# Attention in a macaron block: single score banks and maxima over pairs of banks

## The chip, the core and the metric

The kernel runs on one core of a Trainium2 chip. The metric is the device time of one execution in microseconds. The core has TensorE (matmul and transpose, into PSUM), VectorE, ScalarE, GpSimd and SyncE, which issues the DMAs. PSUM has eight banks; one bank holds 512 float32 columns on each of 128 partitions. PE in the profile is TensorE's matmul, PEld its weight load, DVE VectorE, ACT ScalarE, POOL GpSimd, SP SyncE.

## The reference

The input x is 4 x 2048 x 256. The block computes, in float32,

```
x = x + 0.5 * ffn(layernorm(x))      # gate/up/down with blockwise FP4 quantisation, 256 -> 704 -> 256
x = x + attention(layernorm(x))      # 16 heads of 16 columns, softmax over 2048 keys, w_out
x = x + 0.5 * ffn(layernorm(x))
```

The attention is `softmax(q k^T / 4) v` for each of 4 x 16 = 64 (batch, head) pairs, called heads below, followed by the output projection.

## The kernel before, in words

The phases run one after another: weights, norm, feed-forward, norm, projection, attention (`attend_phase`, L746), output projection, norm, feed-forward. The change lies in the attention phase alone.

Queries and keys are split into three bfloat16 parts each, stacked to 96 rows, so that one bfloat16 matmul of 96 rows gives the score nearly in float32. Three more rows of Q hold minus the maximum of each query (in three bfloat16 parts), against rows of ones in K. So each block of scores is computed twice. First, for the maxima (`unit`, L984): queries on the partitions and keys on the columns, VectorE takes the maximum of each row (L933). A head has 16 x 2048 such rows in 64 units of 128 queries x 512 keys. Later, for the softmax: keys on the partitions and queries on the columns, 99 rows deep, so that the maximum is already subtracted (L1032); ScalarE takes the exponential (L920) into `probs`, and TensorE multiplies by V (`values`, L1002), which also sums the denominators with a column of ones. Each group of scores or maxima is four matmuls with 32 columns of weights each, side by side in the array, that write 32 partitions each of one bank.

A head g goes in 16 rounds kt (128 keys each). A round on TensorE's queue follows `ORDER` (L762): four groups of scores of head g (False, c) and four maxima units of head g+1 (True, c), from round 12 on of head g+2; then the values of the round before. The maxima run LEAD = 16 units ahead. After round 13 (`NEG_AT`) `turn_neg` (L997) transposes minus the maxima of head g+1, VectorE copies them (L946), and SyncE moves them with three DMAs into the rows of Q (L841). VectorE reduces the 16 x 4 partial maxima to minus the maximum at round 11 (L939), GpSimd splits it. In every eighth head, at round 6, VectorE also inverts denominators (L142). When the values of head g-1 are complete, in round 0 of head g, ScalarE copies them from PSUM to `OT` (L912).

PSUM: `ps_s` is four banks, used as two halves of 1024 columns. A half's exponential waits until both its groups are written, and the groups of the next round wait for the exponential of the half that they overwrite. `ps_o` is one bank for the values. `ps_b` is a ring of three single banks (`RING`); each fill takes the next bank, and `take` (L977) lets TensorE wait until the fill three before has been read. The transpose is a fill of this ring too. All orders are written out by hand; each engine has one queue in program order, and semaphores count groups (`scored`), exponentials (`exped`), fills (`bank_full`, `bank_free`) and rounds of values (`pv_done`).

Of the kernel before, what the change touches and what calls it, by code (L numbers as in the profile page):

```python
# [22 lines left out]
ALU = mybir.AluOpType  # L23
ACT = mybir.ActivationFunctionType
# [5 lines left out]
P = 128  # L30
# [715 lines left out]
def attend_phase(nc, m):  # L746
    NH = B * H
    SLOTS = 3
    UNITS = 64
    LEAD = 16  # L750
    HALF = S // 2

    STRIP = 32


    RING = 3
    FILLS = UNITS + 1
    MAX_AT = 11
    NEG_AT = 13
    INVERT_AT = 6  # L760

    ORDER = ((True, 0), (False, 0), (True, 1), (False, 1), (False, 2), (True, 2), (False, 3), (True, 3))  # L762
    with ExitStack() as ctx:
        def sb(name, shape, dt=F32):
            return ctx.enter_context(nc.sbuf_tensor(name, shape, dt))
# [12 lines left out]
        neg_padded = sb("neg_parts", [P, P], BF16)  # L778
        neg_parts = neg_padded[:, 0:3 * KT].rearrange("p (a t) -> p a t", t=KT)
        neg_T = sb("neg_T", [3 * KT, P], BF16)  # L780
        ps_s = ctx.enter_context(nc.psum_tensor("ps_s", [P, 2, HALF], F32))
        ps_o = ctx.enter_context(nc.psum_tensor("ps_o", [P, 512], F32))
        ps_b = ctx.enter_context(nc.psum_tensor("ps_b", [P, RING, 512], F32))

        qk_loaded = [m.qk_loaded0] + [sem(f"qk_loaded{s}") for s in range(1, SLOTS)]
        v_ready, ones_set = sem("v_ready"), sem("ones_set")
# [20 lines left out]
        def fills_to_neg(n):  # L807

            if isinstance(n, int) and n == 0:
                return 1  # L810

            fills = (n - 1) * FILLS + FILLS_AHEAD + 4 * (NEG_AT + 1) + 1
            if isinstance(n, int) and n == NH - 1:
                fills += UNITS - LEAD - 4 * (NEG_AT + 1)
            return fills

        class Ring:
# [13 lines left out]
        def known(g, at_least):  # L831

            return not isinstance(g, int) or g >= at_least

        with nc.Block() as block:
            @block.sync
            def _(sp):
                def neg_rows(n, s):
                    sp.wait_ge(bank_free, fills_to_neg(n))
                    for k in range(3):  # L840
                        sp.dma_start(Q[s][PAIRS + k:PAIRS + k + 1, :].rearrange("o (t q) -> o t q", q=P),  # L841
                                     neg_T[k * KT:(k + 1) * KT, :]).then_inc(neg_loaded, 16)

                def body(g, s):
                    if not isinstance(g, int) or g + 2 < NH:
                        if known(g, 1):
                            sp.wait_ge(scored, g * 2 * KT)
                            load_head(sp, m, Q[(s + 2) % SLOTS], K[(s + 2) % SLOTS], g + 2, qk_loaded[(s + 2) % SLOTS])
                    if known(g, 1):
                        sp.wait_ge(o_kept, g)  # L850
                        store_head(sp, m, g - 1)
                    if known(g, 1) and g % GROUP == 0:
                        spread_denominators(sp, m, g // GROUP - 1)
                    if not isinstance(g, int) or g + 1 < NH:
                        neg_rows(g + 1, (s + 1) % SLOTS)

                for n in range(1, SLOTS):
                    load_head(sp, m, Q[n], K[n], n, qk_loaded[n])
                neg_rows(0, 0)
                heads(sp, body, lambda: None)  # L860
# [45 lines left out]
            @block.scalar  # L906
            def _(act):
                def keep_o(g):
                    act.wait_ge(pv_done, g * KT)
                    if known(g, 2):  # L910
                        act.wait_ge(m.out_moved, (g - 1) * OUT_MOVES * 16)
                    nc.scalar.copy(m.OT[:], ps_o[:]).then_inc(o_kept, 1)  # L912

                def body(g, s):
                    for kt in range(KT):
                        for half in range(2):
                            act.wait_ge(scored, g * 2 * KT + 2 * kt + half + 1)
                            if known(g, 1) or kt >= 2:
                                act.wait_ge(pv_done, g * KT + kt - 1)
                            nc.scalar.activation(probs[:, (2 * kt + half) % 4, :], ps_s[:, half, :], ACT.Exp,  # L920
                                                 scale=float(DH) ** -0.5).then_inc(exped, 1)
                        if kt == 0 and known(g, 1):
                            keep_o(g)

                heads(act, body, lambda: keep_o(NH))

            @block.vector
            def _(dve):
                def unit(ring, s, k):

                    n, bank = ring.next()
                    dve.wait_ge(bank_full, n + 1)
                    nc.vector.tensor_reduce(mx[:, s, k // 4, bass.ds(k % 4, 1)], ps_b[:, bank, :], AX.X, ALU.max).then_inc(bank_free, 1)  # L933

                def minus_max(ring, n, s):

# [4 lines left out]
                def keep_neg(ring, n):  # L941
                    at, bank = ring.next()
                    dve.wait_ge(bank_full, at + 1)
                    if known(n, 1):
                        dve.wait_ge(neg_loaded, n * 16 * NEG_LOADS)
                    nc.vector.tensor_copy(neg_T[:], ps_b[0:3 * KT, bank].bitcast(BF16)[:, 0:P]).then_inc(bank_free, 1)  # L946

                nc.vector.memset(zeros[:], 0.0).then_inc(ones_set, 1)
                nc.vector.memset(neg_padded[:], 0.0).then_inc(ones_set, 1)
# [6 lines left out]
                def body(g, s):  # L956
                    ring = ring_of(g)
                    more, more2 = (not isinstance(g, int) or g + d < NH for d in (1, 2))
                    for kt in range(KT):
                        for j in range(4):  # L960
                            k = LEAD + 4 * kt + j
                            if k < UNITS and more:
                                unit(ring, (s + 1) % SLOTS, k)
                            if k >= UNITS and more2:
                                unit(ring, (s + 2) % SLOTS, k - UNITS)
                        if kt == INVERT_AT and known(g, 1) and g % GROUP == 0:
                            invert_denominators(nc, dve, m, g // GROUP - 1)
                        if kt == MAX_AT and more:
                            minus_max(ring, g + 1, (s + 1) % SLOTS)
                        if kt == NEG_AT and more:  # L970
                            keep_neg(ring, g + 1)
# [4 lines left out]
            def _(pe):  # L976
# [7 lines left out]
                def unit(ring, n, s, k):  # L984

                    if k == 0:
                        if not known(n, SLOTS):
                            pe.wait_ge(rows_set, n + 1)
                        pe.wait_ge(qk_loaded[s], 16 * LOADS * (n // SLOTS + 1) if isinstance(n, int) else (n - s) * (16 * LOADS // SLOTS) + 16 * LOADS)
                    qt, kb = k // 4, k % 4  # L990
                    bank = take(ring)
                    for j in range(0, P, STRIP):
                        last = nc.tensor.matmul(ps_b[j:j + STRIP, bank, :], Q[s][0:PAIRS, qt * P + j:qt * P + j + STRIP],  # L993
                                                K[s][0:PAIRS, kb * 512:(kb + 1) * 512], start=True, stop=True)
                    last.then_inc(bank_full, 1)

                def turn_neg(ring, n):  # L997
                    pe.wait_ge(neg_step, (n + 1) * NEG_STEPS)
                    bank = take(ring)
                    nc.tensor.transpose(ps_b[:, bank].bitcast(BF16)[:, 0:P], neg_padded[:], m.ident_bf[:]).then_inc(bank_full, 1)  # L1000

                def values(g, s, kt):  # L1002

                    pe.wait_ge(exped, g * 2 * KT + 2 * kt + 2)
                    if kt == 0:
                        pe.wait_ge(v_ready, g + 1)
                        if known(g, 1):
# [7 lines left out]
                def body(g, s):  # L1015
# [3 lines left out]
                    for kt in range(KT):  # L1019
                        for maxima, c in ORDER:  # L1020
                            if maxima:
                                k = LEAD + 4 * kt + c
                                if k < UNITS and more:
                                    unit(ring, g + 1, (s + 1) % SLOTS, k)
                                if k >= UNITS and more2:
                                    unit(ring, g + 2, (s + 2) % SLOTS, k - UNITS)
                                continue
                            half = c // 2
                            if c % 2 == 0 and (known(g, 1) or kt >= 1):
                                pe.wait_ge(exped, g * 2 * KT + 2 * kt + half - 1)  # L1030
                            for j in range(0, P, STRIP):
                                last = nc.tensor.matmul(ps_s[j:j + STRIP, half, (c % 2) * 512:(c % 2 + 1) * 512],  # L1032
                                                        K[s][:, kt * P + j:kt * P + j + STRIP],
                                                        Q[s][:, c * 512:(c + 1) * 512], start=True, stop=True)
                            if c % 2:
                                last.then_inc(scored, 1)
                        if kt > 0:
                            values(g, s, kt - 1)
                        elif known(g, 1):
# [133 lines left out]
```

## Time and profile before

| | us |
|---|---|
| median of 3 runs | 4177.33 |
| lowest, highest | 4172.32, 4178.78 |
| the profiled execution, its own time | 4175.14 |
| its span, first to last instruction | 4173.4 |

| engine | busy us | share of the span |
|---|---|---|
| TensorE matmul (PE) | 4028.9 | 97% |
| TensorE weight load (PEld) | 2136.3 | 51% |
| VectorE (DVE) | 3715.4 | 89% |
| ScalarE (ACT) | 2449.2 | 59% |
| GpSimd (POOL) | 1105.3 | 26% |

The attention phase lies between about 860 and 3552 us. Busy time is the union of the records on an engine; consecutive instructions of one engine can overlap, so a mean duration times a count can exceed the busy time. The ends of matmuls are modelled, their starts are not. "idle before" is the time in which an engine had no record before the row, and the arrow names what released it.

### The profile page before, as it was taken

To read this page: it belongs to the slowest core of one execution; us is meant where nothing else is said; L and a number is where in the kernel's file an instruction comes from. 1 tells how busy PE (TensorE), PEld (TensorE's weight loads), DVE (VectorE), ACT (ScalarE), POOL (GpSimd) and SP (SyncE) were. 2 spreads that over 40 slices of the span, in tenths; PEclk is the share of its full clock that TensorE was granted. 3 is DMA by queue.
4 is the path that set the end of the run, shared out by engine and by line. 5 is a ranking of instruction groups with operands and counts; after the bars stand their busy time and mean duration, and the time that the engine had idled before them with its cause. 6 is when DMAs were issued, how large, how long until landed. Compare 5 with 4: busy or idle time off the path is not lost. (4 is left out here: it accounts for less than half of the span.)

```text
span 4173.4 us, 109253 instructions
## 1 busy us (share of the span) xinstructions
PE 4028.9 (97%) x46386; PEld 2136.3 (51%) x46386; DVE 3715.4 (89%) x6349; ACT 2449.2 (59%) x2764; POOL 1105.3 (26%) x1158
## 2 busy tenths in 40 slices
PE   3999999979999999999999999999999999799999
PEld 2777765534444444444444444444444443677776
DVE  7999982679999999999999999999999996699998
ACT  1222225447777777777777777777777778122222
POOL 3888862310000000000000000000000000288886
PEclk7999999989999999999999999999999999999999
DMA  3000003310010001001001101001000100100000
GB/s 133 1 1 1 1 1 111 124 41 20 29 31 29 20 29 31 29 20 40 20 29 31 29 20 40 20 29 32 28 22 27 33 26 9 34 11 21 16 16 21
DMA packets 67121, 125.52 MB, mean 30 GB/s; under 512 B 17104, under 2 KB 46160, under 8 KB 64848
## 3 DMA queue, kind: packets, MB, share of 16 engines
q1 hardware_dynamic: 66640, 118.61, 9.5%
q8 instruction: 363, 5.95, 0.6%
q14 instruction: 118, 0.97, 0.1%
HBM read 72.55 MB, written 36.31 MB: 26 GB/s over the span
## 5 line engine op out<-in xcount | busy, mean ns | idle before, releaser
L933 DVE TENSOR_REDUCE mx<-ps_b 128x1 f32<-128x512 f32 x4032 | 2500.5, 682 | 127.0 <-PE ps_b L993 15.4
L920 ACT ACTIVATE probs<-ps_s 128x1024 f32<-128x1024 f32 x2048 | 1983.9, 1021 | 688.0 <-PE ps_s L1032 687.9
L993 PE MATMUL ps_b<-w_ffn 96*32 96x512 bf16 x10752 | 1070.2, 382 | 14.0 <-DMA w_ffn<-qk_parts_dram 12.1
L1010 PE MATMUL ps_o<-probs,w_qkvT 128*32 128x512 f32 x8192 | 1064.4, 592 | 0.6 <-ACT probs L920 0.6
L1032 PE MATMUL ps_s<-w_ffn 99*32 99x512 bf16 x10752 | 942.5, 379 | 0.6 <-ACT probs L920 0.6
L542 PE MATMUL ps_gu_f<-w_ffn,zT_f 128*128 128x352 f32 x2048 | 636.2, 464 | 10.4 <-DVE h_f L447 9.5
L993 PE MATMUL ps_b<-K,Q 96*32 96x512 bf16 x5376 | 533.3, 380 | 0.2
L993 PEld LDWEIGHTS ps_b<-w_ffn 96*32 96x32 bf16 x10752 | 302.4, 96 | 428.1 <-issue 201.4
L1032 PEld LDWEIGHTS ps_s<-w_ffn 99*32 99x32 bf16 x10752 | 304.6, 97 | 412.9 <-issue 198.7
L1032 PE MATMUL ps_s<-Q,K 99*32 99x512 bf16 x5632 | 493.5, 381 | 1.7 <-ACT probs L920 1.7
L877 POOL TENSOR_TENSOR neg_parts<-neg_max,zeros 128x16 bf16<-128x16 f32 x64 | 14.1, 221 | 1815.8 <-issue 1718.2
L542 PEld LDWEIGHTS ps_gu_f<-w_ffn,zT_f 128*128 128x128 f32 x2048 | 383.6, 192 | 205.8 <-ACT zT_f L399 12.0
L1010 PEld LDWEIGHTS ps_o<-probs,w_qkvT 128*32 128x32 f32 x8192 | 261.1, 111 | 201.1 <-ACT probs L920 1.6
L552 PE MATMUL ps_dn_f<-w_ffn,hT_f 128*128 128x256 f32 x1536 | 353.0, 379 | 5.3 <-ACT hT_f L404 5.3
L552 PEld LDWEIGHTS ps_dn_f<-w_ffn,hT_f 128*128 128x128 f32 x1536 | 291.4, 190 | 65.6 <-ACT hT_f L404 6.8
L1032 PEld LDWEIGHTS ps_s<-Q,K 99*32 99x32 bf16 x5632 | 159.6, 98 | 224.1 <-issue 102.9
L399 ACT COPY zT_f<-ps_T_f 128x256 f32<-128x256 f32 x128 | 47.6, 372 | 367.7 <-PE ps_T_f L534 346.5
L993 PEld LDWEIGHTS ps_b<-K,Q 96*32 96x32 bf16 x5376 | 151.3, 96 | 204.0 <-issue 93.7
L408 ACT ACTIVATE z_f<-x_res,shift,rstd 128x256 f32<-128x256 f32 x128 | 76.7, 601 | 246.9 <-POOL z_scaled_f L490 242.0
L504 POOL TENSOR_TENSOR h_rounded_f<-h_scaled_f,h_rounder_f 128x704 f32<-128x704 f32 x128 | 215.5, 1684 | 21.9 <-DVE h_scaled_f L481 21.9
L865 POOL COPY w_qkvT<-v_then_heads 128x256 f32<-128x256 f32 x64 | 25.4, 397 | 717.3 <-PE ps_o L1010 717.3
L464 DVE TENSOR_TENSOR h_scaled_f<-h_f,h_inv_f 128x704 f32<-128x704 f32 x128 | 199.7, 1560 | 4.4
(117 smaller groups left out, 3085.4 us busy)
## 6 DMA issues: line engine op xcount, KB each, us to landing
qk_parts_dram<-qk_parts SPq DMA_DIRECT2D x96, 256.0 KB, 2.8
w_ffn<-qk_parts_dram SPq DMA_DIRECT2D x84, 192.0 KB
w_ffn<-qk_parts_dram SPq DMA_DIRECT2D x84, 128.0 KB
x_res<-in_L_attn_x SPq DMA_DIRECT2D x4, 2048.0 KB, 20.2
factor<-denom_dram SPq DMA_DIRECT2D x64, 128.0 KB, 5.1
out<-x_res SPq DMA_DIRECT2D x16, 512.0 KB, 2.7
v_then_heads<-OT SPq DMA_DIRECT2D x224, 32.0 KB
w_ffn<-qk_parts_dram SPq DMA_DIRECT2D x84, 64.0 KB
```

Source lines behind the costliest of these rows:

```text
L399: nc.scalar.copy(zT[:, 1 - q, :], ps_zT).then_inc(zT_kept, 1)
L408: nc.scalar.activation(z[:, q, :], m.x[:, i + 4, :], ACT.Identity, bias=m.shift[:, bass.ds(i + 4, 1)], scale=m.rstd[:, bass.ds(i + 4, 1)]) ...
L464: nc.vector.tensor_tensor(blocks_of(hs[:, q, :]), blocks_of(h[:]), spread(hinv[:], I), ALU.mult).then_inc(h_step, 1)
L504: nc.gpsimd.tensor_tensor(hr[:], hs[:, q, :], hM[:, q, :], ALU.subtract).then_inc(hr_ready, 1)
L542: last = nc.tensor.matmul(ps_gu[:, c, 0:HW], zT[:, q, k * P:(k + 1) * P], m.w_guT[:, k, c * HW:(c + 1) * HW], start=(k == 0), stop=(k == K ...
L552: last = nc.tensor.matmul(ps_dn[:, 1 - q, 0:D], hT[:, 1 - q, c * P:(c + 1) * P], m.w_dnT[:, c, :], start=(c == 0), stop=(c == FC - 1))
L865: nc.gpsimd.tensor_copy(V[s][:, :, 0:DH], m.va.rearrange("p (g k d) -> p g k d", k=KT, d=DH)[:, n]).then_inc(v_ready, 1)
L920: nc.scalar.activation(probs[:, (2 * kt + half) % 4, :], ps_s[:, half, :], ACT.Exp, scale=float(DH) ** -0.5).then_inc(exped, 1)
L933: nc.vector.tensor_reduce(mx[:, s, k // 4, bass.ds(k % 4, 1)], ps_b[:, bank, :], AX.X, ALU.max).then_inc(bank_free, 1)
L993: last = nc.tensor.matmul(ps_b[j:j + STRIP, bank, :], Q[s][0:PAIRS, qt * P + j:qt * P + j + STRIP], K[s][0:PAIRS, kb * 512:(kb + 1) * 512] ...
L1010: last = nc.tensor.matmul(ps_o[32 * c:32 * c + 32, :], V[s][:, kt, :], probs[:, (2 * kt + c // 2) % 4, (c % 2) * 512:(c % 2 + 1) * 512], s ...
L1032: last = nc.tensor.matmul(ps_s[j:j + STRIP, half, (c % 2) * 512:(c % 2 + 1) * 512], K[s][:, kt * P + j:kt * P + j + STRIP], Q[s][:, c * 51 ...
```

## The change

`ps_s` becomes three single banks, used in turn by the groups of scores (group number modulo 3). Each group is signalled by itself, and ScalarE takes one exponential of 512 columns a group. The ring for the maxima becomes two pairs of banks. A unit fills both banks of a pair with 128 queries x 1024 keys, by eight matmuls, and one VectorE reduce takes the two maxima of a pair. There are 32 units a head and two a round; LEAD is 8. The order of a round becomes two groups of scores, a unit, a group of scores, a unit, a group of scores, the values. The transpose takes a pair of banks of the ring and writes the first. The order of work on VectorE, GpSimd and SyncE stays, with its counts adapted.

```diff
-    UNITS = 64
-    LEAD = 16
+    UNITS = 32
+    LEAD = 8
+    S_BANKS = 3
-    RING = 3
+    RING = 2
-    ORDER = ((True, 0), (False, 0), (True, 1), (False, 1), (False, 2), (True, 2), (False, 3), (True, 3))
+    ORDER = ((False, 0), (False, 1), (True, 0), (False, 2), (True, 1), (False, 3))
-        ps_s = ctx.enter_context(nc.psum_tensor("ps_s", [P, 2, HALF], F32))
+        ps_s = ctx.enter_context(nc.psum_tensor("ps_s", [P, S_BANKS, 512], F32))
-        ps_b = ctx.enter_context(nc.psum_tensor("ps_b", [P, RING, 512], F32))
+        ps_b = ctx.enter_context(nc.psum_tensor("ps_b", [P, RING, 2, 512], F32))
...
@@ ScalarE
-                        for half in range(2):
-                            act.wait_ge(scored, g * 2 * KT + 2 * kt + half + 1)
+                        for c in range(4):
+                            at = g * 4 * KT + 4 * kt + c
+                            act.wait_ge(scored, at + 1)
                             if known(g, 1) or kt >= 2:
                                 act.wait_ge(pv_done, g * KT + kt - 1)
-                            nc.scalar.activation(probs[:, (2 * kt + half) % 4, :], ps_s[:, half, :], ACT.Exp,
-                                                 scale=float(DH) ** -0.5).then_inc(exped, 1)
+                            nc.scalar.activation(probs[:, (2 * kt + c // 2) % 4, (c % 2) * 512:(c % 2 + 1) * 512],
+                                                 ps_s[:, at % S_BANKS, :], ACT.Exp, scale=float(DH) ** -0.5).then_inc(exped, 1)
@@ VectorE, unit
-                    nc.vector.tensor_reduce(mx[:, s, k // 4, bass.ds(k % 4, 1)], ps_b[:, bank, :], AX.X, ALU.max).then_inc(bank_free, 1)
+                    nc.vector.tensor_reduce(mx[:, s, k // 2, 2 * (k % 2):2 * (k % 2) + 2], ps_b[:, bank], AX.X, ALU.max).then_inc(bank_free, 1)
@@ TensorE, unit
-                    for j in range(0, P, STRIP):
-                        last = nc.tensor.matmul(ps_b[j:j + STRIP, bank, :], Q[s][0:PAIRS, qt * P + j:qt * P + j + STRIP],
-                                                K[s][0:PAIRS, kb * 512:(kb + 1) * 512], start=True, stop=True)
+                    for half in range(2):
+                        kb = 2 * (k % 2) + half
+                        for j in range(0, P, STRIP):
+                            last = nc.tensor.matmul(ps_b[j:j + STRIP, bank, half, :], Q[s][0:PAIRS, qt * P + j:qt * P + j + STRIP],
+                                                    K[s][0:PAIRS, kb * 512:(kb + 1) * 512], start=True, stop=True)
                     last.then_inc(bank_full, 1)
@@ TensorE, values
-                    pe.wait_ge(exped, g * 2 * KT + 2 * kt + 2)
+                    pe.wait_ge(exped, g * 4 * KT + 4 * kt + 4)
@@ TensorE, a round's scores
-                            half = c // 2
-                            if c % 2 == 0 and (known(g, 1) or kt >= 1):
-                                pe.wait_ge(exped, g * 2 * KT + 2 * kt + half - 1)
+                            at = g * 4 * KT + 4 * kt + c
+                            if at >= S_BANKS:
+                                pe.wait_ge(exped, at - S_BANKS + 1)
                             for j in range(0, P, STRIP):
-                                last = nc.tensor.matmul(ps_s[j:j + STRIP, half, (c % 2) * 512:(c % 2 + 1) * 512],
+                                last = nc.tensor.matmul(ps_s[j:j + STRIP, at % S_BANKS, :],
                                                         K[s][:, kt * P + j:kt * P + j + STRIP],
                                                         Q[s][:, c * 512:(c + 1) * 512], start=True, stop=True)
-                            if c % 2:
-                                last.then_inc(scored, 1)
+                            last.then_inc(scored, 1)
```

## Rows read from the trace of the kernel before

**Rows 1.** Stretches: us, busy of PE, PEld, DVE, ACT, POOL, then clock, DMA.
```profile
2500.00:3500.00 1000.00, 999.78 (x15264) 440.83 (x15260) 955.46 (x1576) 749.50 (x787) 45.01 (x131) 1.00 0.10 27
```

**Rows 2.** Waits of weight loads, 920 to 3500: us in total, times, longest.
```profile
PEld ps_b L993 <- DVE mx L933: 8.4, 21, 0.6
```

**Rows 3.** Order of time, TensorE, one round: start, us, engine, line, operation, count.
```profile
2047.28 0.39 PE L993 MATMUL ps_b<-w_ffn 96*32 96x512 bf16 x4
...
2049.02 1.03 PE L1010 MATMUL ps_o<-probs,w_qkvT 128*32 128x512 f32 x8
2049.88 0.39 PE L993 MATMUL ps_b<-w_ffn 96*32 96x512 bf16 x4
```

**Rows 4.** Order of time around the transpose of a head.
```profile
2043.53 1.04 PE L1010 MATMUL ps_o<-probs,w_qkvT 128*32 128x512 f32 x8
...
2044.66 0.40 PE L993 MATMUL ps_b<-w_ffn 96*32 96x512 bf16 x4
2044.77 0.22 DVE L946 COPY neg_T<-ps_b 48x128 bf16<-48x128 bf16 x1
...
2045.12 15.50 DVE L933 TENSOR_REDUCE mx<-ps_b 128x1 f32<-128x512 f32 x24
```

**Rows 5.** Order of time: two copies of OT, a head apart, and the values before one.
```profile
2051.62 1.03 PE L1010 MATMUL ps_o<-probs,w_qkvT 128*32 128x512 f32 x8
...
2052.80 0.59 ACT L912 COPY OT<-ps_o 128x512 f32<-128x512 f32 x1
...
2094.74 0.59 ACT L912 COPY OT<-ps_o 128x512 f32<-128x512 f32 x1
```

**Rows 6.** Order of time in the last head, which has no maxima beside it.
```profile
3519.94 0.59 ACT L912 COPY OT<-ps_o 128x512 f32<-128x512 f32 x1
3520.41 3.81 ACT L920 ACTIVATE probs<-ps_s 128x1024 f32<-128x1024 f32 x4
...
3524.40 3.77 ACT L920 ACTIVATE probs<-ps_s 128x1024 f32<-128x1024 f32 x4 [0.18 <-PE ps_s L1032]
...
3525.47 0.21 PEld L1032 LDWEIGHTS ps_s<-Q,K 99*32 99x32 bf16 x8 [0.64 <-ACT probs L920]
```

**Rows 7.** The page's groups of instructions: busy, mean ns, idle before.
```profile
L933 DVE TENSOR_REDUCE mx<-ps_b 128x1 f32<-128x512 f32 x4032 | 2500.5, 682 | 127.0 <-PE ps_b L993 15.4
L920 ACT ACTIVATE probs<-ps_s 128x1024 f32<-128x1024 f32 x2048 | 1983.9, 1021 | 688.0 <-PE ps_s L1032 687.9
```

**Rows 8.** One line of the projection phase: ns min/median/max.
```profile
L704 DVE TENSOR_REDUCE stats<-ps_yT x32: 1223/1224/1226, 733.6 to 830.5; 128x1024 f32 x32
```

**Rows 9.** Order of time: the maximum over a head's parts.
```profile
2039.55 0.22 DVE L939 TENSOR_REDUCE neg_max<-mx 128x16 f32<-128x64 f32 x1
```

**Rows 10.** Order of time around a reciprocal of the denominators.
```profile
1228.11 0.94 DVE L142 RECIPROCAL denom<-denom 128x128 f32<-128x128 f32 x1
...
1228.97 6.10 DVE L933 TENSOR_REDUCE mx<-ps_b 128x1 f32<-128x512 f32 x10
...
1229.18 0.40 PE L1032 MATMUL ps_s<-w_ffn 99*32 99x512 bf16 x4
1229.65 0.10 PEld L993 LDWEIGHTS ps_b<-K,Q 96*32 96x32 bf16 x4 [0.57 <-DVE mx L933]
```

**Rows 11.** Order of time: the units ahead of the first head.
```profile
861.50 9.66 DVE L933 TENSOR_REDUCE mx<-ps_b 128x1 f32<-128x512 f32 x16 [12.51 <-PE ps_b L993]
...
871.61 0.62 PE L993 MATMUL ps_b<-w_ffn 96*32 96x512 bf16 x4 [1.58 <-DMA Q<-neg_T]
```

**Rows 12.** Order of time around the last transpose and the next head's first load.
```profile
3513.50 1.05 PE L1032 MATMUL ps_s<-w_ffn 99*32 99x512 bf16 x16
...
3513.85 1.80 SPq L841 DMA_DIRECT2D Q<-neg_T  x3
...
3514.38 1.03 PE L1010 MATMUL ps_o<-probs,w_qkvT 128*32 128x512 f32 x8
...
3517.14 0.13 PEld L1032 LDWEIGHTS ps_s<-Q,K 99*32 99x32 bf16 x4 [0.41 <-DMA Q<-neg_T]
```

More of the change, by code:

```diff
@@ L810, in fills_to_neg @@
                 return 1
-            fills = (n - 1) * FILLS + FILLS_AHEAD + 4 * (NEG_AT + 1) + 1
+            fills = (n - 1) * FILLS + FILLS_AHEAD + 2 * (NEG_AT + 1) + 1
             if isinstance(n, int) and n == NH - 1:
-                fills += UNITS - LEAD - 4 * (NEG_AT + 1)
+                fills += UNITS - LEAD - 2 * (NEG_AT + 1)
             return fills
@@ L846, in body @@
                         if known(g, 1):
-                            sp.wait_ge(scored, g * 2 * KT)
+                            sp.wait_ge(scored, g * 4 * KT)
                             load_head(sp, m, Q[(s + 2) % SLOTS], K[(s + 2) % SLOTS], g + 2, qk_loaded[(s + 2) % SLOTS])
@@ L945, in keep_neg @@
                         dve.wait_ge(neg_loaded, n * 16 * NEG_LOADS)
-                    nc.vector.tensor_copy(neg_T[:], ps_b[0:3 * KT, bank].bitcast(BF16)[:, 0:P]).then_inc(bank_free, 1)
+                    nc.vector.tensor_copy(neg_T[:], ps_b[0:3 * KT, bank, 0].bitcast(BF16)[:, 0:P]).then_inc(bank_free, 1)
                 nc.vector.memset(zeros[:], 0.0).then_inc(ones_set, 1)
@@ L959, in body @@
                     for kt in range(KT):
-                        for j in range(4):
-                            k = LEAD + 4 * kt + j
+                        for j in range(2):
+                            k = LEAD + 2 * kt + j
                             if k < UNITS and more:
@@ L989, in unit @@
                         pe.wait_ge(qk_loaded[s], 16 * LOADS * (n // SLOTS + 1) if isinstance(n, int) else (n - s) * (16 * LOADS // SLOTS) + 16 * LOADS)
-                    qt, kb = k // 4, k % 4
+                    qt = k // 2
                     bank = take(ring)
-                    for j in range(0, P, STRIP):
-                        last = nc.tensor.matmul(ps_b[j:j + STRIP, bank, :], Q[s][0:PAIRS, qt * P + j:qt * P + j + STRIP],
-                                                K[s][0:PAIRS, kb * 512:(kb + 1) * 512], start=True, stop=True)
+                    for half in range(2):
[3 more added lines that the diff above has]
+                                                    K[s][0:PAIRS, kb * 512:(kb + 1) * 512], start=True, stop=True)
                     last.then_inc(bank_full, 1)
@@ L999, in turn_neg @@
                     bank = take(ring)
-                    nc.tensor.transpose(ps_b[:, bank].bitcast(BF16)[:, 0:P], neg_padded[:], m.ident_bf[:]).then_inc(bank_full, 1)
+                    nc.tensor.transpose(ps_b[:, bank, 0].bitcast(BF16)[:, 0:P], neg_padded[:], m.ident_bf[:]).then_inc(bank_full, 1)
                 def values(g, s, kt):
-                    pe.wait_ge(exped, g * 2 * KT + 2 * kt + 2)
+                    pe.wait_ge(exped, g * 4 * KT + 4 * kt + 4)
                     if kt == 0:
@@ L1021, in body @@
                             if maxima:
-                                k = LEAD + 4 * kt + c
+                                k = LEAD + 2 * kt + c
                                 if k < UNITS and more:
```

## The prediction

> **What bounds the kernel now.** I began with the stretches: inside the attention phase TensorE is busy 999.8 of 1000 us at granted clock 1.00, that is 2.4 GHz, while VectorE has 955 and ScalarE 750 [rows 1]. So the phase goes at TensorE's pace, and only idle TensorE time could be won. Next the waits of the weight loads between 920 and 3500 us: VectorE held them up 21 times, 8.4 us in all, most of it under earlier matmuls [rows 2]. Then the order of time in one round kt: eight groups of four 32-column matmuls (U, a block for the maxima; s, a block of scores), one every 0.217 us, then the values V, 0.868 us to the next group; 2.604 us a round [rows 3]. Once a head the transpose T of minus the maxima stands behind V: V begins at 2043.53 and the next group at 2044.66, so T adds 2044.66 - 2043.53 - 0.868 = 0.26 us [rows 4]. 16 x 2.604 + 0.26 = 41.92; between two copies of OT, one a head, lie 41.94 us [rows 5]. Nothing of size is idle there. The last 20 rounds (kt 12 to 15 of head 62, all of head 63) have no maxima, and go at ScalarE's cycle: four exponentials of 1024 columns every 3.77 + 0.18 = 3.95 us, which is two rounds [rows 6].
>
> VectorE is nearer its limit than its name in the chain tells: one reduce of 512 columns lasts 0.682 us [rows 7], and sixteen back to back took 9.66 us, a start every 0.60 us; four are 2.40 of the 2.604 us.
>
> **The change part by part.** *Work of TensorE:* groups and columns stay the same; 2.604 us a round if nothing waits. In the new order a round has s0 at 0, s1 at 0.217, the pair U0 at 0.433 and 0.650, s2 at 0.867, U1 at 1.083 and 1.300, s3 at 1.517, V at 1.733.
>
> *Maxima in pairs.* The reduce over 2 x 512 columns exists already in the projection: 1.224 us, 32 times, within 3 ns [rows 8]. Back to back the 512 form overlaps its successor by 0.68 - 0.60 = 0.08 us; I take the same, so 1.14 us from start to start, 2.28 a round. A reduce begins 0.46 us after its last group starts (2044.66 to 2045.12) [rows 4]. Thus U0 is ready at 0.650 + 0.46 = 1.11 and its reduce ends at 2.33; that of U1 starts at 1.11 + 1.14 = 2.25 and ends at 3.475. A freed bank lets a weight load start some 0.05 us later (ScalarE's end at 3525.42, the load at 3525.47 [rows 6]): 3.525. The pair after next in these banks is due at 2.604 + 1.083 = 3.687. So in an ordinary round nothing stalls, with 0.16 us to spare; without any overlap of the reduces 0.08. The maximum at kt 11 (0.22 us [rows 9]) fits into the 0.24 us that VectorE then idles until the next pair is ready at 3.71, and costs nothing.
>
> *The transpose.* Here the two-deep ring bites. T takes a whole pair of banks, as the third fill of kt 13. U0 of kt 14 then needs the pair that U1 of kt 13 had, which is free at 3.525. TensorE reaches it at 1.733 + 0.868 + 0.26 + 0.433 = 3.294. Stall 0.23 us. Before, with three single banks, the group followed T at once [rows 4]. It happens in the 62 heads that still have maxima at kt 14: 14.4 us. From above, without overlap of the reduces, 0.315 us or 19.5; from below nothing, if the pair comes free earlier than I think; I take 14.4, as its terms have rows. It is not given back: TensorE has no idle time to catch up in.
>
> *The reciprocal of the denominators*, in 7 heads at kt 6 on VectorE: next reduce 0.86 us after its start; TensorE's group came at 1229.65 for a due 1229.40, so 0.25 us [rows 10]. New: it starts about 3.39, the reduce of U0 at 4.25 instead of 3.71, that of U1 ends at 4.25 + 1.14 + 1.224 = 6.61, free at 6.66, due at 2 x 2.604 + 1.083 = 6.29: stall 0.37. 7 x 0.12 = 0.9 us; bounds 0 and 2.
>
> *Exponentials on 512 columns.* No row has this form. On 1024 columns it is 1.021 us [rows 7], and four back to back are 3.77 us, so one every 0.92; ScalarE's copy of 512 columns is 0.59, and what follows it starts 0.47 later (3519.94 to 3520.41) [rows 6]. So I put an exponential at 0.594 us (the copy's, and 1.021 less 512 columns of 0.92 us / 1024 gives 0.56), with the next 0.51 behind it; bounds 0.47 and 0.594. In a full round they start at 0.44, 0.95, 1.45 and 1.96 and each score bank is free at least 0.4 us before the block after next but two needs it (s3, due 1.517, needs the end of s0's, 1.03). At a head's start the copy of OT waits for V: V at 2051.62, copy at 2052.80 [rows 5], 1.18 later; so at 2.91, then the exponential of s0 from 3.38 to 3.98, free at 4.03, and s3 is due at 4.12: no cost, 0.09 us to spare. The finer blocks bring TensorE nothing in these rounds either, since ScalarE was never the one it waited for.
>
> *The last 20 rounds.* The old cycle can be read: a pair's end, + 0.05, two groups 0.434, V 0.868, one group 0.217, 0.44 to ScalarE's start, and 1.94 of exponentials: 3.95 us for two rounds, as measured [rows 6]. In the new one s3 waits for the exponential of s0 of its own round, and s0 of the next round stands behind s3 and V: 0.594 + 0.05 + 0.217 + 0.868 + 0.44 = 2.17 us a round against 1.976. 20 x 0.194 = 3.9 us slower. Bounds: 0, and 8.0 if the exponentials don't overlap (4 x 0.594 = 2.38 a round).
>
> *What costs nothing.* The eight first pairs: the old sixteen ended at 871.16 and TensorE stood until 871.61 for rows of Q [rows 11]; the new ones end at about 861.9 + 7 x 1.14 + 1.22 = 871.1. Without that cover it would be under 1 us either way. Minus the maxima: the copy of T starts when U1's reduce is over, at about 3.44 instead of 2.97, ends at 3.66; the last of three DMAs has landed 3.3 us after the first issue (3513.85 to the load at 3517.14 [rows 12]), so by 7.0; head g+1 asks at 2.864 + 0.23 + 2 x 2.604 = 8.3, less some 0.3 that a weight load runs ahead, in the new order with scores first. 1 us to spare; if it were gone, each 0.1 us costs 6 us over 63 heads. SP's queue has the same instructions behind the same events. More waits on TensorE and ScalarE are all met in advance.
>
> Sum: 14.4 + 0.9 + 3.9 = 19.2 us on the profiled execution's 4175.1 (span 4173.4): 4194.3. The median of the runs shown is 2.2 above that execution, so I forecast 4196.5.
>
> A rule of the Trainium skill speaks against smaller instructions. The rows above show exponentials overlapping by 0.10 us and reduces by 0.08 [rows 6, 11]. The page "VectorE: DVE Perf Modes", section "The TRN2 errata", says that an instruction pays a fixed latency whatever its size, 172 cycles on ScalarE for a PSUM source, between instructions, so that cutting work into small tiles pays it for each. By it an exponential on 512 columns is (172 + 512) / 1.2 GHz = 0.57 us and four are 2.28 us, which would make the last rounds 2.28 instead of 2.17 and the sum 21.4 instead of 19.2. The trace gives a shorter start-to-start time, so the sum above goes by the rows.
>
> **The rivals.** (A) *The pair is free in time, and T costs no more than before.* Decides: whether U1 of kt 13 is freed before 3.29 of its round. For it: TensorE's modelled ends are loose by tenths of a us, and the stall is only 0.23. Against: two reduces of 1.224 us one behind the other after 1.11 cannot end before 3.4. Left are 0.9 + 3.9: 4182, not slower within what a measurement of this kernel can tell (0.2%, 8.4 us).
> (B) *ScalarE doesn't overlap its short exponentials.* 2.38 us a round, still under 2.604, but s0's after the copy ends at 2.91 + 0.593 + 0.594 = 4.10, + 0.05 against 4.12: 0.03 x 63 = 1.9 us; last rounds 8.0. 14.4 + 0.9 + 1.9 + 8.0 = 25: 4202. For it: twice the instructions and waits. Against: the rows of overlap.
> (C) *VectorE becomes the bound of every round*, from the point where the 0.16 us to spare are gone. If the pair's reduce were 0.1 us longer (1.32, every 1.24), U1's pair is free at 3.725 against 3.687: 0.038 us in 1004 rounds, 38 us, and the stall at T 0.43 us, 27: 4177 + 38 + 27 + 5 = 4247. For it: at 2.28 us of work in 2.604, the ring of two leaves little. Against: 32 reduces of that form within 3 ns, two engines at work beside them.
> (D) *Groups come closer together in the new order*, because kinds alternate less: at 512 columns / 2.4 GHz = 0.2133 a round would be 2.56, 44 us less over 1004 rounds: 4152 with the stalls. Against: four score groups in a row in the tail took 0.88 us (3513.50 to V at 3514.38 [rows 12]), 0.22 each, no alternation at all.
>
> **How the numbers follow.** Forecast 60%, with its own range 4186 to 4207; A 17%, B 9%, C 8%, D 6%. Slower: nearly all of the forecast, B and C, 0.76; same: A and an edge of the forecast, 0.18; faster: D, 0.06. The range runs from 4180, which leaves out D and a part of A, to 4222, which takes in B and the upper bounds (19.5 + 2 + 8 + 2 gives 4209) and a mild C; the strong C is out.
>
> **What would show it.** Round 2.60 us in mid-phase and TensorE again over 99% busy: C and D wrong. A gap of about 0.23 us on TensorE before the first U of kt 14, released by VectorE, and heads of 42.2 instead of 41.94 us: the main step; no gap means A. Reduces of 1.22 us, 2016 of them. Exponentials of 0.59 us; last rounds of 2.17 us: the third term; 2.38 means B. I am wrong altogether if mid-phase rounds differ from 2.60 us, or if TensorE waits for ScalarE or for Q's rows in them.

## The result, and the profile after

The changed kernel takes 4186.61 us (median of 12 runs, 4183.72 to 4189.16) against 4176.05 before: a ratio of 1.0025, 95% interval 1.0016 to 1.0034, so 10.4 us slower (6.7 to 14.2). I had forecast 19.2 us slower. The profiled executions differ by 8.5 us in their span (4181.9 against 4173.4), and by 9.4 us between the first copy of OT and the last, 918.54 to 3560.45 against 918.7 to 3551.24.

The page after, part 5 (busy, mean ns, idle before), the lines that answer to [rows 7]:

```profile
L935 DVE TENSOR_REDUCE mx<-ps_b 128x2 f32<-128x1024 f32 x2016 | 2373.2, 1219 | 264.4 <-PE ps_b L997 264.3
L922 ACT ACTIVATE probs<-ps_s 128x512 f32<-128x512 f32 x4096 | 2174.4, 599 | 487.9 <-PE ps_s L1036 482.6
```

The reduce over a pair is what the projection's rows promised, 1.22 us, and the exponential of 512 columns is 0.60. On these reduces VectorE works 127 us less and waits 137 us more; in ordinary rounds nobody was waiting for it. The same stretch as [rows 1] in the changed kernel:

```profile
2500.00:3500.00 1000.00, 999.28 (x15226) 444.60 (x15220) 904.92 (x811) 818.90 (x1544) 45.27 (x131) 1.00 0.11 27
```

TensorE still seems never idle. The waits of the weight loads between 920 and 3500 us, the first of which answers to [rows 2]:

```profile
PEld ps_b L997 <- DVE mx L935: 37.0, 78, 0.6
PEld ps_s L1036 <- ACT probs L922: 499.5, 1636, 0.3
```

VectorE now holds loads up 78 times instead of 21. The second line looks like what I had named as a sign of being altogether wrong, TensorE waiting for ScalarE. It is not: these loads pause for 0.3 us under the matmuls of the values, as they do in the kernel before, where the view names no releaser (567 us in 1823 times). The group behind the values starts 0.86 us after them as before (1230.12 to 1230.98 below, 2049.02 to 2049.88 in [rows 3]).

The order of time around a transpose, which answers to [rows 4], shows what TensorE's busy share hides:

```profile
2044.29 0.61 PE L997 MATMUL ps_b<-w_ffn 96*32 96x512 bf16 x8
...
2044.94 2.35 DVE L935 TENSOR_REDUCE mx<-ps_b 128x2 f32<-128x1024 f32 x2 [0.24 <-PE ps_b L997]
...
2045.59 1.04 PE L1014 MATMUL ps_o<-probs,w_qkvT 128*32 128x512 f32 x8
...
2046.72 0.61 PE L1036 MATMUL ps_s<-Q,K 99*32 99x512 bf16 x8
...
2047.22 0.21 DVE L948 COPY neg_T<-ps_b 48x128 bf16<-48x128 bf16 x1
2047.35 0.12 PEld L997 LDWEIGHTS ps_b<-w_ffn 96*32 96x32 bf16 x8 [0.51 <-DVE mx L935]
2047.35 0.62 PE L997 MATMUL ps_b<-w_ffn 96*32 96x512 bf16 x8
```

The two reduces of round 13 end at 2044.94 + 2.35 = 2047.29, the pair is written again from 2047.35. Two groups of scores after 2046.72 it was due at 2046.72 + 0.4335 = 2047.15: 0.20 us of waiting, most of it invisible in TensorE's busy time, because the modelled end of the group before lies at 2047.33. The starts tell the wait, not TensorE's idle column.

Copies of OT a head apart, which answer to [rows 5]: 42.03 us in this head instead of 41.94.

```profile
2012.94 0.59 ACT L913 COPY OT<-ps_o 128x512 f32<-128x512 f32 x1 [0.29 <-PE ps_o L1014]
2054.97 0.59 ACT L913 COPY OT<-ps_o 128x512 f32<-128x512 f32 x1 [0.29 <-PE ps_o L1014]
```

Over all heads the median is 42.07 us against 41.99. The stall alone would have made it 42.19, the 42.2 of the forecast; something gave 0.12 us back in each head. It is in the ordinary rounds: averaged over the starts of 65 to 69 equal rounds between 1960 and 2160 us, a round is 2.598 us against 2.6046, and over all 920 or so undisturbed rounds of the phase 2.5978 against 2.6057. TensorE in two of them, answering to [rows 3]:

```profile
1228.38 0.61 PE L1036 MATMUL ps_s<-w_ffn 99*32 99x512 bf16 x8
1228.81 0.61 PE L997 MATMUL ps_b<-K,Q 96*32 96x512 bf16 x8
1229.25 0.40 PE L1036 MATMUL ps_s<-w_ffn 99*32 99x512 bf16 x4
1229.46 0.61 PE L997 MATMUL ps_b<-K,Q 96*32 96x512 bf16 x8
1229.90 0.40 PE L1036 MATMUL ps_s<-w_ffn 99*32 99x512 bf16 x4
1230.12 1.04 PE L1014 MATMUL ps_o<-probs,w_qkvT 128*32 128x512 f32 x8
1230.98 0.61 PE L1036 MATMUL ps_s<-w_ffn 99*32 99x512 bf16 x8
1231.41 0.61 PE L997 MATMUL ps_b<-K,Q 96*32 96x512 bf16 x8
...
1232.35 0.61 PE L997 MATMUL ps_b<-K,Q 96*32 96x512 bf16 x8
```

The last line is the stall behind a reciprocal, [rows 10]: due at 1232.07, so 0.28 us, where the kernel before had 0.25.

The last rounds, [rows 6], in the changed kernel (TensorE, then ScalarE):

```profile
3551.31 0.40 PE L1036 MATMUL ps_s<-Q,K 99*32 99x512 bf16 x4 [0.27 <-ACT probs L922]
3551.53 1.03 PE L1014 MATMUL ps_o<-probs,w_qkvT 128*32 128x512 f32 x8
3552.39 0.82 PE L1036 MATMUL ps_s<-Q,K 99*32 99x512 bf16 x12
3553.49 0.40 PE L1036 MATMUL ps_s<-Q,K 99*32 99x512 bf16 x4 [0.27 <-ACT probs L922]
```
```profile
3526.68 32.59 ACT L922 ACTIVATE probs<-ps_s 128x512 f32<-128x512 f32 x60
```

A round is 2.18 us (3551.31 to 3553.49), and each time s3 starts when ScalarE has freed its bank. ScalarE's exponentials start every (32.59 - 0.60) / 59 = 0.542 us on average. The one row of 60 looks like unbroken work, but this view joins instructions with less than 0.15 us between them. The busy time of the same stretch tells more:

```profile
3527.00:3559.00 32.00, 27.87 (x348) 8.44 (x348) 0.00 (x0) 30.40 (x60) 0.00 (x0) 1.00 0.03 6
```

ScalarE is busy for 30.40 of 32 us, so it idles some 0.11 us in each round. The single records say where: start to start 0.494, 0.478, 0.478 and then 0.730 us, the last one with 0.11 us of idle time in it, before the exponential of s0. ScalarE was not at its limit.

The account of the 9.4 us: stalls behind the transpose 62 x 0.198 = 12.3; the transpose itself starts 0.013 us later behind the values than before on average, 0.8; ordinary rounds 1004 x 0.0079 = 7.9 less (6.6 by the short stretch alone); reciprocals 7 x 0.03 = 0.2; last rounds 3.75 (39.77 + 34.26 us in the last two intervals between copies against 38.98 + 31.3). Together 9.15.

### The profile page after: what moved, and what is told of

The parts are those of the page before. It is cut to its first block and busy times, and to the rows that moved or that the text cites. A ratio compares the mean times of both kernels' runs of the same rounds, so it can differ in the third digit from the quotient of the medians.

```text
span 4181.9 us, 111329 instructions
## 1 busy us (share of the span) xinstructions
PE 4033.0 (96%) x46386; PEld 2132.5 (51%) x46386; DVE 3586.6 (86%) x4333; ACT 2640.3 (63%) x4812; POOL 1106.3 (26%) x1158
## 5 line engine op out<-in xcount | busy, mean ns | idle before, releaser
L935 DVE TENSOR_REDUCE mx<-ps_b 128x2 f32<-128x1024 f32 x2016 | 2373.2, 1219 | 264.4 <-PE ps_b L997 264.3
L922 ACT ACTIVATE probs<-ps_s 128x512 f32<-128x512 f32 x4096 | 2174.4, 599 | 487.9 <-PE ps_s L1036 482.6
L997 PE MATMUL ps_b<-w_ffn 96*32 96x512 bf16 x10752 | 831.1, 380 | 14.6 <-DMA w_ffn<-qk_parts_dram 12.3
L878 POOL TENSOR_TENSOR neg_parts<-neg_max,zeros 128x16 bf16<-128x16 f32 x64 | 14.2, 222 | 1843.3 <-issue 1746.0
L997 PEld LDWEIGHTS ps_b<-w_ffn 96*32 96x32 bf16 x10752 | 297.5, 96 | 315.0 <-DVE mx L935 31.3
L997 PE MATMUL ps_b<-K,Q 96*32 96x512 bf16 x5376 | 412.5, 379 | 0.7
```

The lines of the kernel that those rows point to most:

```text
L922: nc.scalar.activation(probs[:, (2 * kt + c // 2) % 4, (c % 2) * 512:(c % 2 + 1) * 512], ps_s[:, at % S_BANKS, :], ACT.Exp, scale=float(DH ...
L935: nc.vector.tensor_reduce(mx[:, s, k // 2, 2 * (k % 2):2 * (k % 2) + 2], ps_b[:, bank], AX.X, ALU.max).then_inc(bank_free, 1)
L997: last = nc.tensor.matmul(ps_b[j:j + STRIP, bank, half, :], Q[s][0:PAIRS, qt * P + j:qt * P + j + STRIP], K[s][0:PAIRS, kb * 512:(kb + 1) ...
```

## The experiments

Times are medians; ratios are against the kernel before on the same chip, with their 95% intervals. The theory was that the pair displaced by the transpose makes the stall, that three score banks make the slow last rounds, and that neighbours of one kind make the short rounds; each had a rival in its expectation.

**Transpose into a score bank** (label e1). From the changed kernel:

```diff
-                    bank = take(ring)
-                    nc.tensor.transpose(ps_b[:, bank, 0].bitcast(BF16)[:, 0:P], neg_padded[:], m.ident_bf[:]).then_inc(bank_full, 1)
+                    at = turned_into(n)          # (n - 1) * 64 + 4 * (NEG_AT + 1) + 2; 2 for n = 0
+                    if n > 0:
+                        pe.wait_ge(exped, at - S_BANKS + 1)
+                    nc.tensor.transpose(ps_s[:, at % S_BANKS].bitcast(BF16)[:, 0:P], neg_padded[:], m.ident_bf[:]).then_inc(neg_full, 1)
...
+                            if more and at == turned_into(g + 1):
+                                pe.wait_ge(neg_kept, g + 2)
```

> The changed kernel, but the transpose of minus the maxima goes into a score bank (the one that the third group of scores of the next round uses) and is no fill of the ring any more. Theory: the transpose took one of only two pairs of banks, so the first pair of round 14 waited 0.198 us in 62 heads; here no gap there (values, 0.98 us, transpose, 0.16, two groups of scores 0.43, pair) and 62 x 0.198 = 12.3 us less than the changed kernel's 4186.6: 4174. Rival: the gap has another cause (the reduce of the second pair of round 13 is late whatever takes the banks): the gap stays 0.2 us and the time 4186.

4176.58 us, 1.0003 (0.9994 to 1.0012); heads 41.89 us instead of 42.07. Its order of time around a transpose:

```profile
1961.75 0.23 PE L1000 MATMUL ps_s<-ident_bf,neg_parts 128*128 128x128 bf16 x1
...
1961.91 0.61 PE L1036 MATMUL ps_s<-w_ffn 99*32 99x512 bf16 x8
...
1962.35 0.61 PE L991 MATMUL ps_b<-K,Q 96*32 96x512 bf16 x8
```

0.44 us from the scores to the pair: the gap is gone, and by the medians 10 of the 12.3 us (7.6 us between the first and the last copy of OT in the profiled executions). Part of the rest came back as a new wait: at a head's start TensorE's loads waited 18 times for the three rows of Q, 11.1 us in all and up to 1.54, where the changed kernel had 5 such waits, 1.9 us in all. Behind the longest one the load started 5.3 us after the first of the three DMAs was issued, against 3.3 in [rows 12]. My margin of 1 us holds for the usual landing, not for the slow ones.

**Exponentials and order of the change, single banks for the maxima** (e3). From the changed kernel:

```diff
-    UNITS = 32
-    LEAD = 8
+    UNITS = 64
+    LEAD = 16
-    RING = 2
+    RING = 4
-    ORDER = ((False, 0), (False, 1), (True, 0), (False, 2), (True, 1), (False, 3))
+    ORDER = ((False, 0), (False, 1), (True, 0), (True, 1), (False, 2), (True, 2), (True, 3), (False, 3))
-        ps_b = ctx.enter_context(nc.psum_tensor("ps_b", [P, RING, 2, 512], F32))
+        ps_b = ctx.enter_context(nc.psum_tensor("ps_b", [P, RING, 512], F32))
```

> The changed kernel with its scores and exponentials, but the maxima in a ring of four single banks with one reduce of 512 columns each, TensorE's order of groups unchanged (s s U U s U U s). Theory: the transpose then displaces one bank of four and nothing waits: no gap, round 2.598 us as in the changed kernel (neighbours set it, not pairs), last rounds 2.18 us: 4174. Rival on the spacing: if pairs shorten the round, it goes back to 2.605 and the time is 4181. Rival on VectorE: its 2.40 us of work a round instead of 2.28 lets it fall behind: waits on it in ordinary rounds, above 4186.

4175.17 us, 1.0000 (0.9991 to 1.0009). The same four banks, singly instead of in pairs, have no stall behind the transpose (0.444 us from scores to maxima), and the deeper ring hides most of the reciprocals too (a head with one is 41.99 us long instead of 42.35). VectorE, with more work, was not waited for. The round is 2.601 us, between 2.598 and 2.605: so against this kernel the pairs give some 2 to 3 ns a round, and the order gives the rest. Both theories of the short rounds were half right.

**The kernel before, its order regrouped** (e2):

```diff
-    ORDER = ((True, 0), (False, 0), (True, 1), (False, 1), (False, 2), (True, 2), (False, 3), (True, 3))
+    ORDER = ((True, 0), (True, 1), (False, 0), (False, 1), (False, 2), (False, 3), (True, 2), (True, 3))
```

> The kernel before, with its order in a round made U U s s s s U U values (two changes between maxima and scores instead of six). Theory: a group that follows one of the other kind starts 0.2185 us after it, one of the same kind 0.2155, so 4 x 3 ns = 12 ns a round: a round of 2.592 instead of 2.6046 us, 1004 rounds, 12 us less than before: 4164. Rival: the shorter rounds of the changed kernel (2.598) come of pairs, with half the signals and waits, not of the neighbours: the round stays 2.605 and the time 4176. Second rival: three banks don't carry two groups of maxima in a row and VectorE's waits appear: slower than 4180.

4168.51 us, 0.9985 (0.9976 to 0.9994): 6.3 us faster than before by one line, where I had expected 12. The direction of the theory holds, its size does not. A round is 2.594 us instead of the 2.592 expected, 11.5 us in all. Part goes elsewhere: a round with a transpose loses 0.033 us more than before (2.0 us in all), half of it ahead of the transpose, and a head with a reciprocal is 0.38 us longer than its neighbours instead of 0.22 (1.1 us). Between the first and the last copy of OT this execution is 7.8 us shorter.

**Values before the last scores** (e4), in the 20 rounds without maxima, from the changed kernel:

```diff
                             at = g * 4 * KT + 4 * kt + c
+                            if c == 3 and bare(g, kt):      # head 63, or head 62 from round 12
+                                past_values(g, s, kt)
...
+                        if not bare(g, kt):
+                            past_values(g, s, kt)
```

> The changed kernel, but in the 20 rounds without maxima (kt 12 to 15 of head 62, all of head 63) the values come before the fourth group of scores. Theory: these rounds last 2.18 us because the chain exponential of s0, s3, values, next s0 closes on itself; with the values ahead of s3 it does not, and ScalarE's own pace of four exponentials, 4 x 0.52 = 2.08, is left: 20 x 0.10 = 2.0 us less than 4186.6: 4184.6, the rounds 2.08 to 2.10 us in the trace. Rival: ScalarE's 512-column instructions themselves need 2.18 us a round: the round and the time stay.

4184.54 us, 1.0024 (1.0015 to 1.0034). The time looks like the forecast, but 1.0024 cannot be told from the changed kernel's 1.0025, and the trace shows no gain: the rounds stay at 2.18 us (3551.41 to 3553.59). A time alone would have misled me.

```profile
3551.41 0.40 PE L1047 MATMUL ps_s<-Q,K 99*32 99x512 bf16 x4 [0.27 <-ACT probs L922]
3551.64 1.03 PE L1014 MATMUL ps_o<-probs,w_qkvT 128*32 128x512 f32 x8
3552.50 0.82 PE L1047 MATMUL ps_s<-Q,K 99*32 99x512 bf16 x12
3553.59 0.40 PE L1047 MATMUL ps_s<-Q,K 99*32 99x512 bf16 x4 [0.27 <-ACT probs L922]
```

Moving V only changes which group stands before it. The chain exponential n-3, group n, V, group n+1, exponential n+1 spans four groups, a round, wherever V stands. ScalarE's idle 0.11 us a round already speaks against its being at its own limit; the next run settles it.

**Exponentials of 512 in four banks** (e5), from the regrouped kernel before, its maxima untouched:

```diff
+    S_BANKS = 4
-        ps_s = ctx.enter_context(nc.psum_tensor("ps_s", [P, 2, HALF], F32))
+        ps_s = ctx.enter_context(nc.psum_tensor("ps_s", [P, S_BANKS, 512], F32))
...
+                            nc.scalar.activation(probs[:, (2 * kt + c // 2) % 4, (c % 2) * 512:(c % 2 + 1) * 512],
+                                                 ps_s[:, at % S_BANKS, :], ACT.Exp, scale=float(DH) ** -0.5).then_inc(exped, 1)
```

> The regrouped kernel before (U U s s s s U U values), with exponentials of 512 columns in four single banks, maxima as before in three. It isolates the splitting of the exponentials. Theory: the last rounds of the changed kernel (2.18 us) close the chain exponential n-3, group n, values, group n+1, exponential n+1, which is one round long with three banks wherever the values stand (so putting them before s3 left it at 2.18); with four banks the chain spans five groups and binds no more. Left is ScalarE's own pace, four in 2.04 to 2.08 us: last rounds 2.06 instead of 1.976, + 1.7 us on the regrouped kernel's 4168.5: 4170; mid-phase heads as there, 41.83. Rival: ScalarE itself needs 2.18 us for four with their waits: last rounds 2.18, 4172.6.

4168.19 us, 0.9985 (0.9976 to 0.9994), the same as with 1024 columns. Its last rounds, TensorE:

```profile
3521.65 1.03 PE L1012 MATMUL ps_o<-probs,w_qkvT 128*32 128x512 f32 x8
3522.51 1.27 PE L1034 MATMUL ps_s<-Q,K 99*32 99x512 bf16 x16
3523.61 1.03 PE L1012 MATMUL ps_o<-probs,w_qkvT 128*32 128x512 f32 x8
```

1.96 us a round, and the last interval between copies is 31.3 us as with exponentials of 1024, against 34.26 with three banks. Here ScalarE is at its limit, busy for 18.00 of 18 us:

```profile
3522.00:3540.00 18.00, 17.54 (x224) 5.30 (x220) 0.00 (x0) 18.00 (x38) 0.00 (x0) 1.00 0.01 2
```

So it does a short exponential every 0.49 us, and the third term is the missing fourth bank. In the kernel's time splitting costs nothing, but only because the kernel before lost as much by waiting. ScalarE itself needs 1.96 us for four short exponentials and 2 x 0.92 = 1.84 for two long ones; with its waits the kernel before took 1.976 us a round.

**The two units of a round next to each other** (e7), from the changed kernel:

```diff
-    ORDER = ((False, 0), (False, 1), (True, 0), (False, 2), (True, 1), (False, 3))
+    ORDER = ((False, 0), (False, 1), (True, 0), (True, 1), (False, 2), (False, 3))
```

> The changed kernel with the two units of a round next to each other (s s UU UU s s values). It has two changes of kind a round instead of four, and takes away the slack of the ring. Theory of the ring: in the changed kernel the second pair of a round is free 3.06 us after the first matmul of the first pair (2044.29 to 2047.35); here it is needed after 0.433 + 2.594 = 3.03: a stall of 0.03 us in each of 1004 rounds, 33 us, less 5 us from the neighbours: 4186.6 - 5 + 33 = 4215, rounds of 2.63 us with waits for VectorE in nearly all, while VectorE works 2.28 us of each. Rival (the ring has more slack than that): rounds of 2.593, 4181.

4205.51 us, 1.0073 (1.0060 to 1.0087): 31 us over before, 20 over the changed kernel by the two ratios, where I had 28. Nearly every round waits now. The weight loads' waits between 920 and 3500 us in this kernel, where [rows 2] has 8.4 us and 21 times:

```profile
PEld ps_b L997 <- DVE mx L935: 340.2, 966, 0.8
```

A round is 2.622 us, 0.028 of it between the two pairs (0.8925 us over four groups instead of 0.8645): the ring's arithmetic was right to 0.005 us. The rest of the difference is the stall at the transpose, which falls to 0.16. This is rival C, made real in a mild form: the ring of two pairs carries the round only if the pairs are spread over it. Without its waits this round is 2.594 us, no shorter than e8's with single banks in the same order, so what pairs give in the spacing is not shown beyond the comparison with e3.

**Transpose in two strips** (e6), from the regrouped kernel before:

```diff
-                    nc.tensor.transpose(ps_b[:, bank].bitcast(BF16)[:, 0:P], neg_padded[:], m.ident_bf[:]).then_inc(bank_full, 1)
+                    for j in range(0, 3 * KT, STRIP):
+                        last = nc.tensor.transpose(ps_b[j:j + STRIP, bank].bitcast(BF16)[:, 0:P], neg_padded[:, j:j + STRIP], m.ident_bf[:])
+                    last.then_inc(bank_full, 1)
```

> The regrouped kernel before, with the transpose of minus the maxima as two matmuls with 32 columns of weights each (the 48 rows that are used lie in the first 64), like all its neighbours, instead of one with 128. Theory: of the 0.27 to 0.30 us that it adds to a head, 0.11 ahead of it and 0.10 behind it are weight loads of whole width that cannot run under a neighbour's matmul; strips can: 0.06 instead of 0.30, 63 x 0.2 = 13 us less than 4168.5: 4156, the fastest. Rival: the wait is for the values' last matmuls and not for a weight load: less than 3 us gained.

4170.03 us, 0.9988 (0.9979 to 0.9997): nothing gained, heads 41.88. Its order of time:

```profile
2000.78 0.22 PE L1001 MATMUL ps_b<-ident_bf,neg_parts 128*32 128x128 bf16 x1
2000.81 0.38 PE L993 MATMUL ps_b<-w_ffn 96*32 96x512 bf16 x2
...
2001.16 0.21 DVE L946 COPY neg_T<-ps_b 48x128 bf16<-48x128 bf16 x1
2001.30 0.10 PEld L993 LDWEIGHTS ps_b<-w_ffn 96*32 96x32 bf16 x4 [0.38 <-DVE mx L933]
```

The first maxima follow the transpose within 0.06 us, but the second group waits until 2001.30 for VectorE. The time saved in one place was lost a group later, because the ring of three had no slack for it.

**Four single banks, regrouped** (e8), **and with strips** (e9), from e3:

```diff
-    ORDER = ((False, 0), (False, 1), (True, 0), (True, 1), (False, 2), (True, 2), (True, 3), (False, 3))
+    ORDER = ((False, 0), (False, 1), (True, 0), (True, 1), (True, 2), (True, 3), (False, 2), (False, 3))
```

> The changed kernel's scores (three banks, exponentials of 512), maxima in a ring of four single banks, order s s U U U U s s values: two changes of kind a round. Theory: a change of kind costs TensorE 2.4 to 3 ns, so a round of 2.594 instead of 2.601 with the same banks in the order s s U U s U U s: 61 heads x 0.11 = 7 us less than that kernel's 4175.2, so 4168; last rounds stay at 2.18. Rival: four maxima groups in a row outrun VectorE's 0.60 us a reduce even with four banks: waits on it in every round and over 4175.

4168.56 us, 0.9986 (0.9977 to 0.9995), heads 41.80, round 2.594: as expected.

> The same with the transpose in two strips of 32 columns of weights. With three single banks the strips took 0.25 us off the transpose, and the second group of maxima behind it waited as long for VectorE, 0 gained. Theory: that wait is the ring's, so with four banks the gain stays: the transpose adds 0.06 instead of 0.29 us a head, 62 x 0.23 = 14 us less than the same without strips: 4154, heads of 41.56 us between copies of OT. Rival: the next stop on the way is the DMA of minus the maxima, which has 0.5 us to spare at a head's start: some heads wait for it and 3 to 10 us come back; second rival: the strips gain nothing here either and heads stay at 41.79.

4156.60 us, 0.9957 (0.9944 to 0.9971), 17.9 us faster than before: the fastest version. Heads are 41.59 us. The order of time around its transpose:

```profile
1993.29 1.08 PE L1014 MATMUL ps_o<-probs,w_qkvT 128*32 128x512 f32 x8
1994.15 0.39 PE L1036 MATMUL ps_s<-w_ffn 99*32 99x512 bf16 x2
1994.15 0.22 PE L1003 MATMUL ps_b<-ident_bf,neg_parts 128*32 128x128 bf16 x1
...
1994.59 1.14 PE L995 MATMUL ps_b<-w_ffn 96*32 96x512 bf16 x16
```

Scores and the four groups of maxima follow at once: 1.30 us from the values to the maxima, as in a round without a transpose. Over all heads a round with a transpose is 0.05 us longer than one without, against 0.30 in e8. Rival one was there too, in small: 13 loads waited for the rows of Q, 11 us under matmuls for the most part; five heads took 0.25 to 0.75 us longer.

## Why the prediction was right, and what was mis-sized

*What bounds.* Right: TensorE's sequence sets the phase. VectorE's 0.12 us less work a round bought nothing.

*The transpose and the ring of two.* Right in mechanism and place; 0.198 us instead of 0.232, because a reduce begins 0.65 us after its pair's first matmul (2044.29 to 2044.94) and not 0.217 + 0.46. 12.3 us instead of 14.4. e1 and e3 take the stall away in two different manners. Rival A is out.

*The last rounds.* 3.75 us instead of 3.9, 2.18 us a round instead of 2.17. e4 and e5 show the chain: it depends on the number of banks, not on ScalarE's pace (rival B) or the place of the values. I had named s3 and s0, which holds in this order; in general it is the group before the values and the group behind them.

*The reciprocals.* 0.28 us against 0.25 before where both were read, 0.2 us in sum instead of 0.9; the lengths of the seven heads give 0.4.

*The step that was wrong* is "Work of TensorE: groups and columns stay the same; 2.604 us a round if nothing waits". A round became 2.598 us, 7.9 us in the phase, and with it the forecast of 19.2 would have been 11.3. The term was put at nothing. I had it as rival D, at over five times its size and as all or nothing, and dismissed it on four score groups in 0.88 us. That stretch was a bad witness twice over: its starts are told to 0.01 us, too coarse for an effect of 3 ns, and it stands behind a transpose, where the first spacing is 0.227 and the second 0.220 us after nearly every transpose of this kernel.

The single records of many rounds of the kernel before would have shown it. From the first group of a stretch of one kind to the next group, whatever its kind, are 0.2186 us; from the second group of the stretch to the next, 0.2150. So the extra 3.6 ns do not lie where the kind changes, as I wrote in the expectation of e2, but one group later: 0.2186 between the two neighbouring scores, 0.2150 from the second to the maxima behind it. Each stretch of one kind pays once, so counting changes gives the same sum. Rounds by changes of kind within them: 2.605 with six, 2.601 with four, 2.594 with two; the count alone would make the last 2.591, but there one of the long spacings is 0.2200. What in the array or the queue makes it so stays open: the kinds differ in rows (96 and 99), in moving tensor and in waits, and no run parts these.

*What costs nothing.* The lead held. The rows of Q held in the changed kernel (5 waits, 1.9 us; before 5, 2.3 us), but with less room than I said: e1 and e9 paid there.

*The rule on short instructions.* An exponential on 512 columns lasts 0.60 us in mid-phase and starts every 0.49 in e5's last rounds, where each is recorded as 0.87 long. The Trainium skill's "VectorE: DVE Perf Modes", section "The TRN2 errata", gives 172 cycles and one for each column; worked out from it, an estimate, that is 0.57 us for one and 2.28 for four. Its sentence that the cost lies between instructions is written of SBUF latency; the prediction carried it over to a PSUM source. Here four take 1.96 us. The difference between two short ones (0.98) and one long one (0.92) leaves 0.06 us that each instruction pays from start to start, where 172 cycles would be 0.14. So the direction of the rule holds on ScalarE, most of the fixed part is hidden between neighbours, and the measurement decides.

## What to carry to other kernels

When buffers are merged into fewer, larger ones, look for the rare small user of the same ring: it takes a whole large buffer and turns a depth of two into one. Count the chain that closes through n buffers in groups, not in rounds; moving an instruction within it changes nothing, one more buffer removes it. Where an engine is never idle, measure its own spacing over many rounds before calling it constant: in e2 a new order of the same instructions was worth 6 us, over half of what the edit itself cost, and a saving holds only if the ring behind it has slack.

## What the runs showed of the hardware

A transpose with weights of full width between matmuls of 32-column strips costs TensorE 0.27 to 0.30 us; as two strips about 0.05 (e9), where their weight loads run under the values' matmuls. VectorE starts reduces of 2 x 512 PSUM columns every 1.14 us, with 1.22 for one. TensorE can be waiting where its records show no gap: between 2500 and 3500 us of the changed kernel it idles for 0.72 us, though some 24 transposes with 0.2 us of waiting behind each lie there. ScalarE starts an exponential of 512 PSUM columns every 0.49 us and one of 1024 every 0.92, while they last 0.60 and 1.02.
